# Turning the linear queries and the local queries ahead of the linear keys, and projecting attention's output ahead of the MLP's first output products

## The chip, the cores and the metric

One core of a Trainium2 chip runs the whole program. The metric is the device time of one execution in microseconds; a kernel's time is the median of several runs. Five engines work side by side and wait for each other by semaphores: TensorE (PE; its weight loads are shown apart as PEld), VectorE (DVE), ScalarE (ACT), GpSimd (POOL) and SyncE (SP), which starts the DMAs.

## What is computed

The input is 4096 tokens of 256 numbers. Two things are computed from the normalised input and put together:

```python
xn = layernorm(x)
# linear attention, 16 heads of 32, in chunks of 128 tokens with a carried state
q, k = softmax(ln(xn) @ Wq + bq), softmax(ln(xn) @ Wk + bk)      # per head
v, p = split(ln(xn) @ W_in)
k = (1 - smear) * k + smear * k_previous_token
attn = tril((q / s) @ (k / s).T * decay_mask)
s_out = ln(silu(p) * (attn / attn.sum()) @ v @ W_out)
# two layers of local attention (8 heads of 64, windows of 128) with a gated MLP
for l in range(2):
    q, k, v = split(shift(x) @ wqkv[l])
    q, k = rotary(l2norm(q) * qs, l2norm(k) * ks)
    x = x + softmax(local q @ k.T) @ v @ wo[l]
    h = layernorm(shift(x)) * g + b
    a, gate = split(h @ w1[l] + b1[l]); x = x + (a * gelu(gate)) @ w2[l] + b2[l]
out = x_in + s_out * silu(x)
```

## The kernel before

Work is cut into windows of 128 tokens; 32 windows in each of two layers make 64 units. The program is a software pipeline of 67 iterations. Iteration i projects unit i (queries, keys, values of the local attention), attends for unit i-1 and runs the MLP of unit i-2; in layer 1 a last stage finishes unit i-3. The linear attention is spread over the same iterations, one chunk of 128 tokens for every two of them: an odd iteration runs its first part (`one`: projections, softmax, turning queries and keys, scores), the even one behind it the second (`two`: outputs, state, gate, output projection). So every odd iteration from 1 to 63 has a `one`, 32 in all. Most iterations run in loops of two bodies each, an even and an odd one.

Every engine has its own queue, with the order written out by hand in a function `body` for each; an engine takes the next instruction only when the one before has been issued and its waits are met. `Steps` counts an engine's signals: the names are in the order in which they are given, and `at(name, unit)` is the count to wait for.

A matmul wants its contracted index on the partitions, so queries and keys are turned by TensorE (`transposes`, L1530, four blocks of 128x128 into one PSUM bank; the profile shows them under L1533) and copied to SBUF by ScalarE (`copy`, shown under L793). At the end of an odd iteration TensorE's order is:

1. the linear keys into `mix_bank[0]`, waiting for `kadd` (L1431 on VectorE: this token's share of the keys plus that of the token before, both in `mix_work`) and `v`;
2. the local queries (`turn_q`), waiting for `rot` (L1421, the rotation's sum) and for ScalarE's copy of the values out of the same bank (`v_loc`);
3. the linear queries into `mix_bank[1]`, waiting for the softmax's exponentials;
4. two of the six output products of the MLP (`mlp_out(m, 0, 2)`, tiles `w_s`, `hid`), waiting for `a0` (L1279 on VectorE, `gated`);
5. the output projection of the local attention (`out_projection`, tiles `wo_s`, `oT`), waiting for `lb` (L1236);
6. the local keys (`turn_k`), waiting for `knorm` (L1443, the rotated keys times their inverse norms) and for `ql` (L1243, the low half of the turned local queries, which frees the bank);
7. the linear scores, the other MLP products, and the next unit's x.

VectorE's order over the same time is `kadd`, `lb`, `gated`, `knorm`, `ql`, in layer 0 the statistics of the next x, the MLP's last gates (L1132), `residual` (L1124, reads the output projection), `kl` (L1243 on kT, behind ScalarE's copy of the turned local keys), then the linear scores' decays and, in the next iteration, the local scores (L1048). GpSimd's order is `k_dec` (L738, waits for `kadd`), in layer 0 up to iteration 30 the root of the next x's norm (`norm1`, L755), `qT_dec` (L758, waits for ScalarE's copy of the turned linear queries), the root for the local queries' norms (L663) and `x1b` (L767). `qT_dec` is read by the next iteration's linear outputs.

Of the kernel before, what the change touches and what calls it, by code (L numbers as in the profile page):

```python
# [30 lines left out]
P = 128  # L31
# [14 lines left out]
MG = ME // P  # L46
# [126 lines left out]
def build(nc, x_d, in_w, in_b, q_w, q_b, k_w, k_b, out_w, out_b, W_in, W_out, Wq, bq, Wk, bk,  # L173
# [9 lines left out]
    with ExitStack() as ctx:  # L183
        def sb(name, shape):
            return ctx.enter_context(nc.sbuf_tensor(name, shape, F32))
# [7 lines left out]
        def sem(name):  # L193
            return ctx.enter_context(nc.semaphore(name))
# [52 lines left out]
        qk = mix_work[:, 0:2 * ME]  # L247
# [9 lines left out]
        qT_mix = sb("qT_mix", [P, MG, P])  # L257
# [5 lines left out]
        kT_mix = sb("kT_mix", [P, MG, P])  # L263
# [59 lines left out]
        mix_bank = bank[0:2]  # L323
# [4 lines left out]
        score_bank = [mix_bank[0], mix_bank[1], att_bank[0], att_bank[2]]  # L328


        mix_pe = Steps(sem("mix_pe"), "q k v kt qt s0 s1 s2 s3 p o0 o1 gt wout")
        state_pe = Steps(sem("state_pe"), "st0 st1")
        state_dve = Steps(sem("state_dve"), "st0 st1")
        state_pool = Steps(sem("state_pool"), "sdec")
        rows_pe = Steps(sem("rows_pe"), "xt")
        rows_dve = Steps(sem("rows_dve"), "xl")
        mix_act = Steps(sem("mix_act"), "xt exp kt qt tanh gt")
        mix_dve = Steps(sem("mix_dve"), "q k max sum kinv kw v kadd "
                        "s2 qsum qeps s3 s0 s1 p den0 rec0 o0 den1 rec1 o1 go "
                        "ystat yaggr yvar")  # L340
# [101 lines left out]
        def linear(i):  # L442


            odd, n = i.c == 1, i.low // 2
            return (Chunk(i.k, n) if odd and n < NW else None,
                    Chunk(i.k - 1, n - 1) if not odd and 1 <= n < NW + 1 else None,
                    Chunk(i.k - 1, n - 1) if odd and 1 <= n < NW + 1 else None)
# [6 lines left out]
        def streams(i):  # L455

            return (i if i.low < UNITS else None,
                    i.back(1) if 1 <= i.low < UNITS + 1 else None,
                    i.back(2) if 2 <= i.low < UNITS + 2 else None,
                    i.back(3) if i.low >= NW + 3 else None)  # L460
# [330 lines left out]
        def _(act):  # L791
            def copy(out, in_):
                return act.activation(out, in_, ACT.Copy)  # L793
# [75 lines left out]
            def body(i):  # L869
                proj, a, m, f = streams(i)  # L870
                one, two, y = linear(i)
# [92 lines left out]
                if m is not None:  # L964
                    last_gates(m)
                if one is not None:
                    act.wait_ge(mix_pe.sem, mix_pe.at("kt", one))
                    copy(kT_mix[:, :, :], mix_bank[0][:, :].rearrange("p (g i) -> p g i", g=MG))\
                        .then_inc(mix_act.done("kt"), 1)
                if proj is not None:  # L970
                    act.wait_ge(proj_pe.sem, proj_pe.at("qt", proj))
                    copy(halved(qT[:, 0, :, :]), proj_bank[:, :].rearrange("p (g i) -> p g i", g=HP))\
                        .then_inc(proj_act.done("qt"), 1)
                if one is not None:
                    act.wait_ge(mix_pe.sem, mix_pe.at("qt", one))
                    copy(qT_mix[:, :, :], mix_bank[1][:, :].rearrange("p (g i) -> p g i", g=MG))\
                        .then_inc(mix_act.done("qt"), 1)
                if proj is not None:
                    act.wait_ge(proj_pe.sem, proj_pe.at("kt", proj))
                    copy(halved(kT[:, 0, :, proj.parity, :]), proj_bank[:, :].rearrange("p (g i) -> p g i", g=HP))\  # L980
# [7 lines left out]
                if one_next is not None:  # L988
                    turned_rows(one_next)

            iterations(act, body)


# [525 lines left out]
        def _(pe):  # L1519
            def mm(out, lhsT, rhs, first, last):  # L1520
                return pe.matmul(out, lhsT, rhs, start=first, stop=last)  # L1521

            def mm3(out, left, right, first, last):

                for n, (a, b) in enumerate(((1, 0), (0, 1), (0, 0))):
                    ins = pe.matmul(out, halved(left[:, a]), halved(right[:, b]), start=first and n == 0,  # L1526
                                    stop=last and n == 2)
                return ins

            def transposes(out, parts):  # L1530

                for j, part in enumerate(parts):
                    ins = pe.transpose(out[:, j * P:(j + 1) * P], part, ident)  # L1533
                return ins
# [72 lines left out]
            def hidden(m, b, at, first, count):  # L1607

                for j in range(count):
                    for c in range(DC):  # L1610
                        ins = mm(b[:, (at + j) * P:(at + j + 1) * P], w1_s[:, c, (first + j) * P:(first + j + 1) * P],
                                 hT_n[:, c, :], c == 0, c == DC - 1)
                return ins

            def out_projection(a, b):
                if window(a).low == 0:
                    pe.wait_ge(setup_dve.sem, setup_dve.at(f"wo_{layer(a)}", ONCE))
                pe.wait_ge(att_dve.sem, att_dve.at("lb", a))
                for g in range(HP):
                    ins = mm3(b[:, 0:D], oT[:, :, g, :], wo_s[:, :, g, :], g == 0, g == HP - 1)  # L1620
                ins.then_inc(att_pe.done("wo"), 1)

            def turn_q(u):

                pe.wait_ge(proj_act.sem, proj_act.at("v", u))
                pe.wait_ge(proj_dve.sem, proj_dve.at("rot", u))
                transposes(proj_bank, [rot[:, g * P:(g + 1) * P] for g in range(HP)])\
                    .then_inc(proj_pe.done("qt"), 1)
# [33 lines left out]
            def mlp_out(m, first, last):  # L1662

                if first == 0:
                    if window(m).low == 0:
                        pe.wait_ge(w2_loaded, 16 * W2_DMAS * (layer(m) + 1))
                    pe.wait_ge(mlp_dve.sem, mlp_dve.at("a0", m))
                if last > 4:
                    pe.wait_ge(mlp_dve.sem, mlp_dve.at("ga", m))
                for j in range(first, last):  # L1670
                    ins = mm(mlp_bank[1][:, 0:D], hid[:, j, :], w2_s[:, j, :], j == 0, j == HC - 1)
                if last == HC:
                    ins.then_inc(mlp_pe.done("w2"), 1)
# [42 lines left out]
            def body(i):  # L1716
                u, a, m, f = streams(i)
                one, two, y = linear(i)
# [91 lines left out]
                if m is not None and one is None and i.low != UNITS:  # L1810
                    mlp_out(m, 0, 2)
                if one is not None:
                    pe.wait_ge(mix_dve.sem, mix_dve.at("kadd", one))
                    pe.wait_ge(mix_dve.sem, mix_dve.at("v", one))
                    transposes(mix_bank[0], [qk[:, ME + g * P:ME + (g + 1) * P] for g in range(MG)])\
                        .then_inc(mix_pe.done("kt"), 1)
                if u is not None:
                    turn_q(u)
                if one is not None:
                    pe.wait_ge(mix_act.sem, mix_act.at("exp", one))  # L1820
                    pe.wait_ge(mix_dve.sem, mix_dve.at("k", one))
                    transposes(mix_bank[1], [qk[:, g * P:(g + 1) * P] for g in range(MG)])\
                        .then_inc(mix_pe.done("qt"), 1)
                    if m is not None:
                        mlp_out(m, 0, 2)
                if a is not None:
                    out_projection(a, att_bank[1])
                if i.low == UNITS:

                    hidden(m, mlp_bank[0], 2, 4, 2).then_inc(mlp_pe.done("ga"), 1)  # L1830
                    mlp_out(m, 0, 2)
# [24 lines left out]
                if two is not None:  # L1856
# [10 lines left out]
                    ins.then_inc(mix_pe.done("wout"), 1)  # L1867

            iterations(pe, body)


# [23 lines left out]
```

## Time and profile before

| | |
|---|---|
| median of 3 runs | 1975.97 us (1974.36 to 1982.03) |
| the profiled execution | 1983.42 us |
| its span, first to last instruction | 1981.6 us |
| TensorE busy | 1906.0 us, 96% |
| VectorE busy | 1732.8 us, 87% |
| ScalarE busy | 1224.2 us, 62% |
| GpSimd busy | 1018.6 us, 51% |

Busy time counts an instruction from its start to its end; instructions of one engine overlap by some hundredths of a microsecond at their edges. A bracket behind a row of the timeline is the time for which the engine sat idle before it, and what ended that. The profile is of one execution, the median of others, so times inside the span are compared with the profiled execution.

### The profile page before, as it was taken

The numbers are of one execution on the slowest core, as the hardware profiler recorded it, in microseconds if no ns is written. First come the engines' busy times: TensorE is split into PE (matmuls) and PEld (weight loads), VectorE is DVE, ScalarE is ACT, GpSimd is POOL, SyncE is SP. The second block draws the span as 40 slices with busy tenths as digits, with TensorE's granted clock in tenths as the row PEclk, the third lists the DMA queues.
The fourth block names the chain that finished last, engine by engine and source line by source line (L and its number), as shares of the span: only waits on it lengthen the run. The fifth ranks groups of instructions, "written<-read, shape, count | busy, mean of one in ns | idle before, by whom it ended". The sixth has DMA issues, their size and how long they took to land.

```text
span 1981.6 us, 49031 instructions
## 1 busy us (share of the span) xinstructions
PE 1906.0 (96%) x15178; PEld 1645.8 (83%) x15178; DVE 1732.8 (87%) x5212; ACT 1224.2 (62%) x2926; POOL 1018.6 (51%) x1004
## 2 busy tenths in 40 slices
PE   5899999999999999999999999999999999999998
PEld 3788888888888888888788888888888888888887
DVE  5888899898889898889888898889899898898896
ACT  4565656656656656656666567566566566566564
POOL 2545555556556555555444455454554554454552
PEclk8999999999999999999999999999999999999999
DMA  5010000000000100000111111110111111111101
GB/s 199 20 33 21 29 25 22 30 29 22 25 29 21 32 29 21 26 26 25 65 62 47 40 34 41 34 32 29 42 32 40 37 32 29 40 34 34 37 26 33
DMA packets 81152, 72.76 MB, mean 37 GB/s; under 512 B 13484, under 2 KB 74344, under 8 KB 81096
## 3 DMA queue, kind: packets, MB, share of 16 engines
q1 hardware_dynamic: 81096, 72.05, 11.8%
q8 instruction: 31, 0.51, 0.1%
q14 instruction: 25, 0.20, 0.0%
HBM read 42.64 MB, written 16.78 MB: 30 GB/s over the span
## 4 chain that ended last, share of the span: by engine, by line
PE 61%; issue 12%; DVE 12%; ACT 6%; POOL 6%; DVEq 1%; DMA 1%; SPq 0%; POOLq 0%; ACTq 0%
PE bank L1521 36%; PE bank L1526 14%; PE bank L1533 10%; ACT L944 2%; POOL rot_other L707 2%; PE bank L1568 2%; POOL mix_work L715 2%; DVE rot L1413 1%; DVE prob L1048 1%; ACT gel L944 1%; DVE mix_work L1431 1%; POOL small_h L663 1%; DVE sq_sum L1305 1%; POOL small_y L663 1%; DVE mix_work L1112 1%
## 5 line engine op out<-in xcount | busy, mean ns | idle before, releaser
L1521 PE MATMUL bank<-hT_n,w_s 128*128 128x128 f32 x3072 | 402.2, 281 | 1.6 <-ACT hT_n L907 0.9
L1521 PEld LDWEIGHTS bank<-hT_n,w_s 128*128 128x128 f32 x3072 | 364.7, 191 | 35.2 <-issue 21.4
L824 ACT ACTIVATE prob<-prob,row_min 128x256 f32<-128x256 f32 x512 | 256.7, 504 | 171.2 <-DVE row_min L1048 169.6
L1526 PE MATMUL bank<-wqkv_s,xT 128*128 128x512 f32 x1152 | 319.2, 413 | 4.6 <-DVE wqkv_s L1225 1.8
L663 POOL TENSOR_TENSOR inv_norm<-sq_clip,half_neg 128x8 f32<-128x8 f32 x128 | 270.3, 2112 | 55.5 <-DVE sq_clip L1308 55.4
L707 POOL TENSOR_TENSOR rot_other<-raw,rot_t 128x256 f32<-128x256 f32 x256 | 190.2, 774 | 150.0 <-ACT raw L793 150.0
L1526 PEld LDWEIGHTS bank<-wqkv_s,xT 128*128 128x128 f32 x1152 | 207.4, 191 | 53.6 <-DVE wqkv_s L1225 3.8
L1048 DVE CUSTOM_DVE_ANT_0 prob<-bank,table,inv_norm 128x256 f32<-128x256 f32 x512 | 226.5, 479 | 3.9 <-issue 3.6
L1521 PE MATMUL bank<-w_s,hid 128*128 128x256 f32 x768 | 202.3, 387 | 0.0
L793 ACT ACTIVATE pT<-bank 128x512 f32<-128x512 f32 x256 | 139.7, 606 | 30.3 <-PE bank L1533 30.2
L1533 PE MATMUL bank<-table,prob 128*128 128x128 f32 x1024 | 144.9, 274 | 2.3 <-DVE prob L1067 2.3
L1521 PE MATMUL bank<-pT,v_loc 128*64 128x128 f32 x2048 | 140.1, 279 | 5.4 <-ACT pT L793 4.9
L1521 PEld LDWEIGHTS bank<-w_s,hid 128*128 128x128 f32 x768 | 131.5, 191 | 14.7 <-DVE hid L1279 0.2
L1067 DVE TENSOR_SCALAR prob<-prob,row_inv 128x256 f32<-128x256 f32 x384 | 134.1, 391 | 6.8
L1568 PEld LDWEIGHTS bank<-kT,qT 64*128 64x128 f32 x1536 | 100.1, 187 | 45.9 <-issue 29.9
L663 POOL TENSOR_TENSOR small_h<-small_h,half_neg 128x1 f32<-128x1 f32 x64 | 35.4, 553 | 190.3 <-DVE small_h L1292 190.3
L1521 PEld LDWEIGHTS bank<-pT,v_loc 128*64 128x64 f32 x2048 | 109.3, 136 | 23.3 <-issue 9.1
L1568 PE MATMUL bank<-kT,qT 64*128 64x256 f32 x1536 | 126.3, 297 | 1.3 <-DVE row_min L1048 1.0
L793 ACT ACTIVATE oT<-bank 128x256 fp32r<-128x256 f32 x128 | 50.1, 391 | 124.0 <-PE bank L1521 124.0
L1533 PEld LDWEIGHTS bank<-table,prob 128*128 128x128 f32 x1024 | 119.7, 143 | 8.1 <-DVE prob L1067 2.8
L1521 PE MATMUL bank<-v_mix,mix_work 128*128 128x33 f32 x1024 | 124.8, 266 | 0.0
L1521 PEld LDWEIGHTS bank<-v_mix,mix_work 128*128 128x128 f32 x1024 | 124.5, 191 | 0.0
(180 smaller groups left out, 4313.6 us busy)
## 6 DMA issues: line engine op xcount, KB each, us to landing
k_prev<-k_carry SPq DMA_DIRECT2D x32, 224.0 KB, 2.5
x_s<-in_L_attn_x SPq DMA_DIRECT2D x32, 128.0 KB, 2.1
rot_s<-in_rotary SPq DMA_DIRECT2D x64, 64.0 KB, 2.0
rows_normalised<-xh SPq DMA_DIRECT2D x32, 128.0 KB, 1.7
y_n<-rows_normalised SPq DMA_DIRECT2D x32, 128.0 KB, 2.1
x_between_layers<-x SPq DMA_DIRECT2D x32, 128.0 KB, 1.7
s_between_passes<-s_out SPq DMA_DIRECT2D x32, 128.0 KB, 1.7
x_s<-x_between_layers SPq DMA_DIRECT2D x32, 128.0 KB, 2.1
```

Source lines behind the costliest of these rows:

```text
L663: return pool.tensor_tensor(out, in_, half_neg[:, 0:w], ALU.pow)
L707: ins = pool.tensor_tensor(o5[:, a, :, s, :], r5[:, a, :, 1 - s, :], rot_t[:, 2 + a, s, :].unsqueeze(1).to_broadcast([P, H, HD // 2]), ALU ...
L715: pool.tensor_tensor(qk_h, qk_h, qk_max[:, :].unsqueeze(2).to_broadcast([P, 2 * MH, MD]), ALU.subtract).then_inc(mix_pool.done("sub"), 1)
L793: return act.activation(out, in_, ACT.Copy)
L824: ins = act.activation(prob[:, h, :], prob[:, h, :], ACT.Exp, bias=row_min[:, c:c + 1], scale=-1.0, accum_out=row_sum[:, c:c + 1])
L944: ins = act.activation(gel[:, j, :], mlp_bank[0][:, j * P:(j + 1) * P], ACT.Gelu, bias=bias[:, HC + j:HC + j + 1])
L1048: ins = dve.tensor_tensor_reduce(prob[:, h, :], b[:, j * 2 * P:(j + 1) * 2 * P], mask, inv_norm[:, a.parity, h:h + 1], 3e38, ALU.add, ALU.min,
L1067: ins = dve.tensor_scalar(prob[:, h, :], prob[:, h, :], row_inv[:, c:c + 1], None, ALU.mult)
L1521: return pe.matmul(out, lhsT, rhs, start=first, stop=last)
L1526: ins = pe.matmul(out, halved(left[:, a]), halved(right[:, b]), start=first and n == 0, stop=last and n == 2)
L1533: ins = pe.transpose(out[:, j * P:(j + 1) * P], part, ident)
L1568: ins = pe.matmul(banks[s][:, j * 2 * P:(j + 1) * 2 * P], halved(qT[rows, lo_q, h // 2, :]), halved(kT[rows, lo_k, h // 2, :, :].rearrange ...
```

## The change

TensorE turns the linear queries first, then the local queries, then the linear keys. The two MLP output products that stood behind the linear queries in an odd iteration now stand behind the output projection. ScalarE copies the turned tiles out in the new order, and the two signal lists name them so. Nothing is added or left out; even iterations keep their order.

```diff
--- before.py
+++ after.py
@@ -328,13 +328,13 @@
         score_bank = [mix_bank[0], mix_bank[1], att_bank[0], att_bank[2]]
 
 
-        mix_pe = Steps(sem("mix_pe"), "q k v kt qt s0 s1 s2 s3 p o0 o1 gt wout")
+        mix_pe = Steps(sem("mix_pe"), "q k v qt kt s0 s1 s2 s3 p o0 o1 gt wout")
         state_pe = Steps(sem("state_pe"), "st0 st1")
         state_dve = Steps(sem("state_dve"), "st0 st1")
         state_pool = Steps(sem("state_pool"), "sdec")
         rows_pe = Steps(sem("rows_pe"), "xt")
         rows_dve = Steps(sem("rows_dve"), "xl")
-        mix_act = Steps(sem("mix_act"), "xt exp kt qt tanh gt")
+        mix_act = Steps(sem("mix_act"), "xt exp qt kt tanh gt")
         mix_dve = Steps(sem("mix_dve"), "q k max sum kinv kw v kadd "
                         "s2 qsum qeps s3 s0 s1 p den0 rec0 o0 den1 rec1 o1 go "
                         "ystat yaggr yvar")
@@ -964,17 +964,17 @@
                 if m is not None:
                     last_gates(m)
                 if one is not None:
-                    act.wait_ge(mix_pe.sem, mix_pe.at("kt", one))
-                    copy(kT_mix[:, :, :], mix_bank[0][:, :].rearrange("p (g i) -> p g i", g=MG))\
-                        .then_inc(mix_act.done("kt"), 1)
+                    act.wait_ge(mix_pe.sem, mix_pe.at("qt", one))
+                    copy(qT_mix[:, :, :], mix_bank[1][:, :].rearrange("p (g i) -> p g i", g=MG))\
+                        .then_inc(mix_act.done("qt"), 1)
                 if proj is not None:
                     act.wait_ge(proj_pe.sem, proj_pe.at("qt", proj))
                     copy(halved(qT[:, 0, :, :]), proj_bank[:, :].rearrange("p (g i) -> p g i", g=HP))\
                         .then_inc(proj_act.done("qt"), 1)
                 if one is not None:
-                    act.wait_ge(mix_pe.sem, mix_pe.at("qt", one))
-                    copy(qT_mix[:, :, :], mix_bank[1][:, :].rearrange("p (g i) -> p g i", g=MG))\
-                        .then_inc(mix_act.done("qt"), 1)
+                    act.wait_ge(mix_pe.sem, mix_pe.at("kt", one))
+                    copy(kT_mix[:, :, :], mix_bank[0][:, :].rearrange("p (g i) -> p g i", g=MG))\
+                        .then_inc(mix_act.done("kt"), 1)
                 if proj is not None:
                     act.wait_ge(proj_pe.sem, proj_pe.at("kt", proj))
                     copy(halved(kT[:, 0, :, proj.parity, :]), proj_bank[:, :].rearrange("p (g i) -> p g i", g=HP))\
@@ -1810,21 +1810,21 @@
                 if m is not None and one is None and i.low != UNITS:
                     mlp_out(m, 0, 2)
                 if one is not None:
+                    pe.wait_ge(mix_act.sem, mix_act.at("exp", one))
+                    pe.wait_ge(mix_dve.sem, mix_dve.at("k", one))
+                    transposes(mix_bank[1], [qk[:, g * P:(g + 1) * P] for g in range(MG)])\
+                        .then_inc(mix_pe.done("qt"), 1)
+                if u is not None:
+                    turn_q(u)
+                if one is not None:
                     pe.wait_ge(mix_dve.sem, mix_dve.at("kadd", one))
                     pe.wait_ge(mix_dve.sem, mix_dve.at("v", one))
                     transposes(mix_bank[0], [qk[:, ME + g * P:ME + (g + 1) * P] for g in range(MG)])\
                         .then_inc(mix_pe.done("kt"), 1)
-                if u is not None:
-                    turn_q(u)
-                if one is not None:
-                    pe.wait_ge(mix_act.sem, mix_act.at("exp", one))
-                    pe.wait_ge(mix_dve.sem, mix_dve.at("k", one))
-                    transposes(mix_bank[1], [qk[:, g * P:(g + 1) * P] for g in range(MG)])\
-                        .then_inc(mix_pe.done("qt"), 1)
-                    if m is not None:
-                        mlp_out(m, 0, 2)
                 if a is not None:
                     out_projection(a, att_bank[1])
+                if m is not None and one is not None:
+                    mlp_out(m, 0, 2)
                 if i.low == UNITS:
 
                     hidden(m, mlp_bank[0], 2, 4, 2).then_inc(mlp_pe.done("ga"), 1)
```

## Rows read from the trace of the kernel before

**Rows 1.** The page: its first line, and busy time by engine.

```profile
span 1981.6 us, 49031 instructions
...
PE 1906.0 (96%) x15178; PEld 1645.8 (83%) x15178; DVE 1732.8 (87%) x5212; ACT 1224.2 (62%) x2926; POOL 1018.6 (51%) x1004
```

**Rows 2.** Stages: one loop turn of layer 0, one of layer 1; us, busy (instructions).

```profile
848.33:908.19 59.86, 58.93 (x474) 51.08 (x474) 53.57 (x169) 37.63 (x91) 32.95 (x33) 1.00 0.09 26
...
1453.00:1513.10 60.10, 58.83 (x474) 51.05 (x475) 53.81 (x158) 38.10 (x92) 30.83 (x29) 1.00 0.12 35
```

**Rows 3.** Table of waits: us in total, times, longest us.

```profile
PEld bank L1533 <- DVE mix_work L1431: 40.4, 32, 4.1
```

**Rows 4.** The chain that ended last, around one wait: start us, us, what.

```profile
907.52 0.69 DVE mix_work L1431
...
908.34 1.52 PE bank L1533 x12
```

**Rows 5.** Timeline, layer 0, weight loader: start us, us, engine, line, work.

```profile
908.33 0.42 PEld L1533 LDWEIGHTS bank<-table,mix_work 128*128 128x128 f32 x4 [0.89 <-DVE mix_work L1431]
...
909.15 0.47 PEld L1533 LDWEIGHTS bank<-table,mix_work 128*128 128x128 f32 x4
...
909.63 0.73 PEld L1521 LDWEIGHTS bank<-w_s,hid 128*128 128x128 f32 x4
...
910.38 1.58 PEld L1526 LDWEIGHTS bank<-wo_s,oT 128*128 128x128 f32 x12
...
911.91 0.46 PEld L1533 LDWEIGHTS bank<-table,rot 128*128 128x128 f32 x4
```

**Rows 6.** Timeline, the same iteration: VectorE, ScalarE, and the loader at the second scores.

```profile
906.38 1.23 DVE L1421 TENSOR_TENSOR rot<-rot,rot_other 128x1024 f32<-128x1024 f32 x1
...
906.87 0.59 ACT L793 ACTIVATE v_loc<-bank 128x512 f32<-128x512 f32 x1
...
908.12 0.42 DVE L1236 TENSOR_TENSOR oT<-bank,oT 128x256 fp32r<-128x256 f32 x1
...
908.46 1.12 DVE L1279 SCALAR_TENSOR_TENSOR hid<-bank,cols,gel 128x128 f32<-128x128 f32 x4
...
910.14 0.69 DVE L1243 TENSOR_TENSOR qT<-bank,qT 128x512 fp32r<-128x512 f32 x1
...
911.52 0.61 DVE L1132 SCALAR_TENSOR_TENSOR hid<-bank,cols,gel 128x128 f32<-128x128 f32 x2
...
912.21 0.42 DVE L1124 TENSOR_TENSOR x<-bank,xn 128x256 f32<-128x256 f32 x1
...
913.27 0.69 DVE L1243 TENSOR_TENSOR kT<-bank,kT 128x512 fp32r<-128x512 f32 x1 [0.64 <-ACT kT L793]
...
918.28 0.77 PEld L1568 LDWEIGHTS bank<-kT,qT 64*128 64x128 f32 x12 [0.36 <-DVE row_min L1048]
```

**Rows 7.** Timeline, a steady odd iteration of layer 1: loader, GpSimd and VectorE.

```profile
1513.10 0.42 PEld L1533 LDWEIGHTS bank<-table,mix_work 128*128 128x128 f32 x4 [1.25 <-DVE mix_work L1431]
...
1513.13 1.05 POOL L738 TENSOR_TENSOR k_dec<-mix_work,table 128x512 f32<-128x512 f32 x1 [0.51 <-DVE mix_work L1431]
...
1514.26 0.68 DVE L1443 TENSOR_TENSOR rot<-rot,inv_norm 128x512 f32<-128x512 f32 x1
...
1514.91 0.69 DVE L1243 TENSOR_TENSOR qT<-bank,qT 128x512 fp32r<-128x512 f32 x1
...
1515.45 0.74 POOL L758 TENSOR_TENSOR qT_dec<-qT_mix,table 128x256 f32<-128x256 f32 x1 [1.27 <-ACT qT_mix L793]
...
1516.14 1.65 POOL L663 TENSOR_TENSOR inv_norm<-sq_clip,half_neg 128x8 f32<-128x8 f32 x1
1516.70 0.46 PEld L1533 LDWEIGHTS bank<-table,rot 128*128 128x128 f32 x4
```

**Rows 8.** Timeline, an even iteration of layer 0: GpSimd and VectorE at L1443.

```profile
877.99 1.06 POOL L751 TENSOR_TENSOR state<-state,table 128x528 f32<-128x528 f32 x1
...
878.29 1.30 DVE L1443 TENSOR_TENSOR rot<-rot,inv_norm 128x512 f32<-128x512 f32 x1
```

## Prediction

> **What bounds the kernel now.** I read the page first: TensorE is busy 96% of a span of 1981.6 us [rows 1]. So a gain has to be idle time taken from TensorE, or work taken from it, and the change takes no work away: the same instructions stand in another order. Next the table of stages, one loop turn (an even and an odd iteration) of each layer: 59.86 us a turn in layer 0, 60.10 in layer 1, TensorE busy 58.93 and 58.83 [rows 2]. About one microsecond a turn is left. The table of waits says where most of it lies: the weight loader sat 40.4 us in 32 waits before the transposes of L1533, for the write of mix_work by L1431 [rows 3]. L1431 is VectorE's "kadd", the sum of the linear keys; it is there once per odd iteration, so every one of the 32 waits is the wait in front of the linear keys' transposes. The chain that ended last runs through the same place, from kadd straight into these transposes [rows 4]. So the wait is on the path and has to be taken seriously, all the more as VectorE, ScalarE and GpSimd lead up to it without slack.
>
> **Layer 0, TensorE.** In a steady odd iteration [rows 5] the loader idles 0.89 us until 908.33; its last group before the wait has ended at 907.44. Behind the wait stand three groups of four transposes (linear keys, local queries, linear queries), then two of the MLP's output products at 909.63, the output projection at 910.38 and the turn of the local keys at 911.91. The change puts the linear queries and the local queries ahead of the wait. What they need is there: the exponentials and the projection of the linear queries are long done; the local queries' rotation ends at 906.38 + 1.23 = 907.61, and the copy of v_loc, which freed their bank, at 907.46 [rows 6]. The linear keys still cannot start before 908.33, since kadd is unmoved. So the gain is not the 0.89 of idle time but the two groups that no longer stand behind it: 909.15 - 908.33 = 0.82 us. Two groups take 0.82 and the issue gap in front of them ends some 0.05 to 0.15 after 907.44, so they end at 908.31 to 908.41: they may push the keys by up to 0.08. I take 0.77, with 0.72 and 0.82 as ends.
>
> After the keys (0.48 us, 909.15 to 909.63) the output projection begins at about 908.81. It waits for "lb", VectorE's low half of the second attention result, ready at 908.12 + 0.42 = 908.54: no wait. The MLP products follow at about 910.34 (the projection takes 911.91 - 910.38 = 1.53); their "a0" is ready at 908.46 + 1.12 = 909.58. Had they kept their place ahead of the projection they would have met a0 at 908.81 and waited 0.77 us, which would have eaten the gain; this is what the second part of the change is worth, and it costs nothing itself, since the MLP products write another bank and the next of them come only behind the linear scores. The local keys follow 0.75 later at 911.09. They need "ql" on VectorE, which ends at 910.14 + 0.69 = 910.83: just in time, 0.26 us of cover [rows 6].
>
> **Layer 0, VectorE.** A gain of TensorE's is kept only if VectorE can give it too. From 913.27 on it is without a gap, and TensorE waits for it at the second scores (0.36 idle at 918.28) [rows 6]. Between kadd and 913.27 it idles 0.08 us for the output projection (from 911.52 + 0.61 to 912.21) and 0.64 us for ScalarE's copy of the turned local keys (913.27), which itself follows the transposes that now come 0.77 earlier. Earlier by 0.77 the copy ends at about 912.47, and VectorE, done with the residual at 912.55 or 0.07 before it with the overlap of starts that its rows show, goes on at once. So VectorE gives 0.72 plus the overlap: 0.77 goes through. The running maximum, the decays, the next x and the next scores are all behind these on the same queue and move with them; the even iteration behind it is TensorE's own.
>
> **Layer 1, the same and a collision.** The wait is longer (1.25 on the loader at 1513.10, [rows 7]), but the keys again start no earlier than kadd allows, so the saving is again the two groups, 0.82. What differs is GpSimd. Its queue is k_dec (L738), then in layer 0 the root of the next x's norm (waits for VectorE until late), then qT_dec (L758). From iteration 31 on there is no such root. Now qT_dec waits for the linear queries' copy and starts at 1515.45. After the change that copy comes ahead of the keys', near 1513.3, so qT_dec starts as soon as k_dec ends: 1513.13 + 1.05 = 1514.18, or some 0.03 before it, as the back-to-back rows at 1515.45 and 1516.14 overlap. VectorE's scaling of the local keys (L1443) starts at 1514.26, and reads two tiles in SBUF as qT_dec does. The trace shows what that does [rows 8]: at 878.29 the same L1443 began 0.30 us after a GpSimd operation (877.99 for 1.06) and took 1.30 instead of 0.68, as if it had stood until 878.91, 0.14 before GpSimd's operation ended. Behind qT_dec (1514.15 for 0.74) it would stand until 1514.75 and end at 1515.43 instead of 1514.94, 0.49 later. The Trainium skill has this as the shared port pair (SBUF — State Buffer, Who interferes with whom): a VectorE instruction with two SBUF inputs and a GpSimd one that reads SBUF exclude each other for the whole instruction; here the row agrees but for the 0.14, and by the page the delay would be 0.63 and the whole gain some 2 us less. L1443 delayed, "ql" behind it (1514.91, 0.69) ends at 1516.09. TensorE would have come to the local keys at 1516.70 - 0.82 = 1515.88; it goes on 0.06 behind ql, at about 1516.15 to 1516.2. The saving in layer 1 shrinks from 0.82 to **0.52**. Ends: 0.82 if the two miss each other (the margin is 0.11 us), 0.37 if the delay is the longer.
>
> **The sum.** Odd iterations with the root in between: 1 to 29, 15 of them, at 0.77: 11.6 us. Without it: 31 to 63, 17 of them, at 0.52: 8.8 us. Together 20.4 us. The first few iterations wait longer, but the cap of two groups holds for them too. The profiled execution took 1983.42 us (span 1981.6 and 1.8 around it); 1963.0 after, a ratio of 0.9897. The runs' median, 1975.97, is 0.4% below the profiled one; by the ratio it becomes **1955.6 us**.
>
> **Rivals.**
> - *The two operations miss each other in layer 1* (or L1443 wins the port, and GpSimd waits, which costs nothing as qT_dec is needed only in the next iteration). 15 x 0.77 + 17 x 0.82 = 25.5 us: 1950.6. For it: 0.11 us of margin is little. Against: both starts follow from kadd, by fixed durations.
> - *VectorE keeps layer 0's gain.* If residual or the key copy don't come earlier (ScalarE held by its new order of copies), the wait at the second scores grows from 0.36 to over 1.1 us and layer 0 gives nothing: 8.8 us in all, 1967.2, within 0.5%. Against: ScalarE idles before the keys' copy, and its three copies of 0.6 us fit between 908.3 and 910.1. A gain partly lost, 10 us, is the same case.
> - *Slower: L1443 is held through both GpSimd operations.* If the root of 1.65 us that follows qT_dec (1516.14) takes the port first as well, L1443 stands until 1514.15 + 0.74 + 1.65 - 0.14 = 1516.40 and ends at 1517.08; ql behind it ends near 1517.75, and the local keys turn at 1517.8, 1.1 us later than before. 17 x 1.1 - 11.6 = 7 us slower: 1983. It costs layer 1 from a delay of L1443 of about 1.04 on (ql later than 1516.64) and outweighs layer 0's gain from about 1.7 on (1.04 and 11.6 us over 17). Against it: in [rows 8] L1443 got in after one operation, though such a root was next.
>
> **How the numbers follow.** Two medians of this kernel can be told apart from about 0.5%, 9.9 us. Chances: the forecast 0.55 (1952 to 1961), no collision 0.20 (1948 to 1953), VectorE or another engine keeping half or more 0.17 (1962 to 1973), slower 0.05 (1976 to 1990); 0.03 for a gain above 28 us. Leaving out the far ends, the range is 1947.5 to 1968. Faster by over 0.5% (under 1966.1) takes the first two, the surprise and part of the third: 0.83; within 0.5% 0.14; slower 0.03.
>
> **What would show it.** Right: the loader's wait for L1431 falls from 0.89 to below 0.1 us in layer 0 and from 1.25 to some 0.2 in layer 1; the order on TensorE is transposes of mix_work, rot, mix_work, then wo_s, then hid; L1443 takes about 1.17 us in layer 1's odd iterations and 0.68 in layer 0's, and the loader shows a new wait of about 0.3 us for "ql" (qT, L1243) there; a turn takes 59.1 us in layer 0 and 59.6 in layer 1. Wrong: L1443 at 0.68 throughout (then 1950), a wait before the output projection or at the second scores grown by the whole gain, or kadd itself later against the start of its turn, which nothing moved should cause.

## The result

The changed kernel takes 1958.85 us in the median of 4 runs (1955.28 to 1959.92), the kernel before 1977.12 us in runs beside it: a ratio of 0.9902, 95% interval 0.9877 to 0.9926. A second comparison, the same changed kernel on another occasion, gives 1958.05 us and 0.9881 (0.9866 to 0.9896). The forecast was 1955.6 us and a ratio of 0.9897. Of all runs in this document one was slow: e2's at 2101.97 us, at a granted clock of 0.849 where the others have 0.994 to 0.997; its ratio leaves that run out, its median counts it.

The profiled execution has a span of 1958.1 us, 23.5 less than the 1981.6 of [rows 1]. The two lines of its page that answer to those show TensorE's busy time all but unchanged and a shorter span around it:

```profile
span 1958.1 us, 49031 instructions
...
PE 1906.7 (97%) x15178; PEld 1637.0 (84%) x15178; DVE 1741.4 (89%) x5212; ACT 1223.2 (62%) x2926; POOL 1025.9 (52%) x1004
```

The stages, one loop turn of layer 0 and one of layer 1, with the columns of [rows 2]. The turns are 0.62 and 0.64 us shorter, and VectorE's busy time in layer 1 has grown from 53.81 to 54.12:

```profile
835.66:894.90 59.24, 58.81 (x477) 50.94 (x475) 53.66 (x168) 37.51 (x91) 32.94 (x33) 1.00 0.09 27
1435.52:1494.98 59.46, 59.20 (x475) 50.83 (x475) 54.12 (x158) 38.15 (x94) 31.25 (x30) 1.00 0.12 35
```

In the table of waits, the wait for VectorE's L1243 (ql) has grown from 7.3 us in 32 waits (first row), and the one of [rows 3] has shrunk from 40.4 us to a sixth (second row):

```profile
PEld bank L1533 <- DVE qT L1243: 15.1, 50, 1.7
...
PEld bank L1533 <- DVE mix_work L1431: 6.3, 16, 1.3
```

The timeline of a steady odd iteration of layer 0, to be read against [rows 5, 6]. Kadd (L1431) starts at 894.06, and times are best read from there:

```profile
893.90 0.47 PEld L1533 LDWEIGHTS bank<-table,mix_work 128*128 128x128 f32 x4
...
894.06 0.68 DVE L1431 TENSOR_TENSOR mix_work<-mix_work,k_prev 128x512 f32<-128x512 f32 x1
...
894.34 0.47 PEld L1533 LDWEIGHTS bank<-table,rot 128*128 128x128 f32 x4
...
894.87 0.42 PEld L1533 LDWEIGHTS bank<-table,mix_work 128*128 128x128 f32 x4
...
895.25 1.48 PEld L1526 LDWEIGHTS bank<-wo_s,oT 128*128 128x128 f32 x12
...
896.66 0.74 PEld L1521 LDWEIGHTS bank<-w_s,hid 128*128 128x128 f32 x4
...
897.43 0.57 PEld L1533 LDWEIGHTS bank<-table,rot 128*128 128x128 f32 x4
...
898.91 0.69 DVE L1243 TENSOR_TENSOR kT<-bank,kT 128x512 fp32r<-128x512 f32 x1
...
900.95 0.73 POOL L767 TENSOR_TENSOR x1b<-x,b_s 128x256 f32<-128x256 f32 x1
901.21 0.50 DVE L1484 TENSOR_TENSOR q_eps<-qk_sum,head_eps 128x16 f32<-128x16 f32 x1
...
905.24 1.22 PEld L1526 LDWEIGHTS bank<-win_s,xhT 128*128 128x128 f32 x6 [0.55 <-DVE mix_work L1112]
```

The linear queries and the local queries are turned while kadd runs, and the keys follow at +0.81 (894.87), exactly where they stood before (908.33 against 907.52) and without a wait. The local keys' turn starts at +3.37 instead of +4.39, the linear scores behind it at +4.11 instead of +5.01, VectorE's kT at +4.85 instead of +5.75. The row of the scores, before and after:

```profile
912.53 0.98 PEld L1521 LDWEIGHTS bank<-qT_mix,kT_mix 32*128 32x128 f32 x32 [0.17 <-issue]
```

```profile
898.17 0.98 PEld L1521 LDWEIGHTS bank<-qT_mix,kT_mix 32*128 32x128 f32 x32 [0.17 <-issue]
```

Then comes a row that was not forecast: q_eps (L1484), 16 numbers a row, takes 0.50 us instead of 0.17. It began at 901.21, inside GpSimd's x1b (L767, 900.95 to 901.68). The linear projection behind the second scores, at 905.24, waits 0.55 us for VectorE, where before it waited 0.25 (at 919.30).

The same stretch in layer 1, against [rows 7]:

```profile
1494.27 0.42 PEld L1533 LDWEIGHTS bank<-table,rot 128*128 128x128 f32 x4 [0.19 <-DVE rot L1421]
...
1494.94 0.42 PEld L1533 LDWEIGHTS bank<-table,mix_work 128*128 128x128 f32 x4 [0.26 <-DVE mix_work L1431]
...
1494.98 1.05 POOL L738 TENSOR_TENSOR k_dec<-mix_work,table 128x512 f32<-128x512 f32 x1 [0.52 <-DVE mix_work L1431]
...
1495.99 0.73 POOL L758 TENSOR_TENSOR qT_dec<-qT_mix,table 128x256 f32<-128x256 f32 x1
1496.11 1.16 DVE L1443 TENSOR_TENSOR rot<-rot,inv_norm 128x512 f32<-128x512 f32 x1
1496.68 2.10 POOL L663 TENSOR_TENSOR inv_norm<-sq_clip,half_neg 128x8 f32<-128x8 f32 x1
...
1497.19 0.68 DVE L1243 TENSOR_TENSOR qT<-bank,qT 128x512 fp32r<-128x512 f32 x1
...
1497.92 0.42 PEld L1533 LDWEIGHTS bank<-table,rot 128*128 128x128 f32 x4 [0.41 <-DVE qT L1243]
```

The forecast collision is there: qT_dec starts 0.04 before k_dec's end, L1443 begins 0.12 behind it and takes 1.16 us instead of 0.68, and TensorE waits 0.41 us for ql before it can turn the local keys. The wait for kadd (L1431) is 0.26 us, and a short new one of 0.19 stands before the local queries, for the rotation's sum (L1421).

In layer 0 the chain that ended last has left TensorE between kadd and the next iteration. Before, it ran from kadd into the transposes [rows 4]; now it stays on VectorE (start us, us, what):

```profile
894.06 0.14 DVE mix_work L1431
...
895.08 0.82 DVE hid L1279 x4
...
896.03 0.68 DVE rot L1443
896.71 0.60 DVE qT L1243
...
898.61 0.33 DVE x L1124
...
901.21 0.06 DVE q_eps L1484
```

### The profile page after: what moved, and what is told of

It is laid out like the page before. It is cut to its first block, busy times and chain, and to the rows that moved or that the text cites. A ratio compares the mean times of both kernels' runs of the same rounds, so it can differ in the third digit from the quotient of the medians.

```text
span 1958.1 us, 49031 instructions
## 1 busy us (share of the span) xinstructions
PE 1906.7 (97%) x15178; PEld 1637.0 (84%) x15178; DVE 1741.4 (89%) x5212; ACT 1223.2 (62%) x2926; POOL 1025.9 (52%) x1004
## 4 chain that ended last, share of the span: by engine, by line
PE 56%; DVE 16%; issue 13%; ACT 6%; POOL 6%; DVEq 1%; DMA 1%; SPq 0%; POOLq 0%; ACTq 0%
PE bank L1521 34%; PE bank L1526 13%; PE bank L1533 9%; ACT L944 2%; POOL rot_other L707 2%; POOL mix_work L715 2%; PE bank L1568 2%; DVE prob L1048 2%; DVE rot L1413 1%; ACT gel L944 1%; DVE mix_work L1111 1%; DVE mix_work L1112 1%; POOL small_h L663 1%; DVE sq_sum L1305 1%; POOL small_y L663 1%
## 5 line engine op out<-in xcount | busy, mean ns | idle before, releaser
L663 POOL TENSOR_TENSOR inv_norm<-sq_clip,half_neg 128x8 f32<-128x8 f32 x128 | 279.5, 2184 | 52.9 <-DVE sq_clip L1308 52.8
```

The costliest lines, as they stand in the source:

```text
L663: return pool.tensor_tensor(out, in_, half_neg[:, 0:w], ALU.pow)
```

## The experiments

A turn is the time from one start of k_dec (L738) to the next. The table has the steady turns of the profiled executions, and the first turn (iteration 1 to 3). Each ratio is to runs of the kernel before from the same occasion: their median was 1980.33 us beside e1 to e4 and 1980.40 beside e5 to e8, so medians of different occasions are not to be divided by each other.

| kernel | first | layer 0 | layer 1 | median us | ratio (95%) |
|---|---|---|---|---|---|
| before | 62.48 | 59.85 | 60.10 | 1977.12 | 1 |
| before, again (e5) | 62.53 | 59.86 | 60.13 | 1981.08 (1 run) | |
| changed | 59.76 | 59.24 | 59.46 | 1958.85 | 0.9902 (0.9877 to 0.9926) |
| changed, again (e6) | 59.78 | 59.25 | 59.48 | 1958.05 | 0.9881 (0.9866 to 0.9896) |
| turns only (e1) | 60.98 | 59.87 | 60.13 | 1977.7 | 0.9987 (0.9974 to 0.9999) |
| projection only (e2) | 62.49 | 59.83 | 60.10 | 1979.26 | 0.9993 (0.9978 to 1.0007) |
| changed, x1b first (e3) | 59.75 | 58.96 | 59.23 | 1949.03 | 0.9842 (0.982 to 0.9863) |
| changed, root first (e4) | 59.80 | 59.25 | 59.23 | 1954.01 | 0.9867 (0.9846 to 0.9888) |
| before, wait filled (e7) | 59.67 | 59.86 | 60.13 | 1976.58 | 0.9979 (0.9969 to 0.9988) |
| before, x1b first (e8) | 60.42 | 59.85 | 60.10 | 1980.88 | 1.0 (0.9991 to 1.0009) |

### Each half of the change alone

The turns in the new order, the MLP products in their old place. Against the changed kernel:

```diff
-                if a is not None:
-                    out_projection(a, att_bank[1])
                 if m is not None and one is not None:
                     mlp_out(m, 0, 2)
+                if a is not None:
+                    out_projection(a, att_bank[1])
```

> Only the three turns are in the new order; the two MLP products stay ahead of the output projection. Theory (the two halves need each other): the linear keys still start 0.8 us after kadd's start, the MLP products come 0.4 us later and wait some 0.8 us for their first gate products (hid, L1279), so the local keys' turn starts 4.4 us after kadd's start as in the kernel before, and a steady turn takes 59.85 us in layer 0 and 60.1 in layer 1. Only the first turns gain, up to 5 us in all: ratio 0.997 to 1.000. Rival (the new order of the turns is the whole gain, the place of the MLP products is of no matter): turns of 59.2 and 59.5 us, ratio 0.990.

The steady turns did not move at all (59.87 and 60.13). The weight loader's rows in an odd iteration of layer 0, whose kadd starts at 659.59:

```profile
660.40 0.42 PEld L1533 LDWEIGHTS bank<-table,mix_work 128*128 128x128 f32 x4
...
661.70 0.73 PEld L1521 LDWEIGHTS bank<-w_s,hid 128*128 128x128 f32 x4 [0.88 <-DVE hid L1279]
...
663.99 0.46 PEld L1533 LDWEIGHTS bank<-table,rot 128*128 128x128 f32 x4
```

The keys are turned at +0.81 and the products come 0.88 us of waiting later, for the gated products (hid, L1279); the local keys' turn starts at +4.40, where [rows 5] have it (+4.39). The whole gain of the two turns is given back in one wait. In layer 1, L1443 is stretched in this run too (1.15 us), and it costs nothing: ql ends at kadd + 3.73, and TensorE reaches the local keys at + 4.41 anyway.

The other half, in the kernel before:

```diff
                     transposes(mix_bank[1], [qk[:, g * P:(g + 1) * P] for g in range(MG)])\
                         .then_inc(mix_pe.done("qt"), 1)
-                    if m is not None:
-                        mlp_out(m, 0, 2)
                 if a is not None:
                     out_projection(a, att_bank[1])
+                if m is not None and one is not None:
+                    mlp_out(m, 0, 2)
```

> Only the output projection goes ahead of the MLP's first products; the turns keep their old order. Theory (it gives nothing by itself, since TensorE has the same work behind the same wait): turns of 59.7 to 59.85 and 60.0 to 60.1 us, the output projection's 12 loads about 0.1 us shorter as in the changed kernel, ratio 0.998 to 1.000. Rival (the earlier residual is what VectorE needed): VectorE's idle time in front of the residual goes, and a turn gets 0.3 us or more shorter, ratio 0.995 or less.

It gives nothing that can be told from nothing. So neither half has a steady gain, and both together have 0.6 us a turn: the first frees the time, the second lets TensorE use it.

### Taking the collisions away

GpSimd's x1b ahead of qT_dec, in the changed kernel. The edit moves qT_dec and the root that follows it behind x1b:

```diff
                 if i.low + 1 < NW:
                     norm1(i.back(-1))
-                if one is not None:
-                    pool.wait_ge(mix_act.sem, mix_act.at("qt", one))
-                    pool.tensor_tensor(qT_dec[:, :, :], qT_mix[:, 0:MG // 2, :], query_decay,
-                                       ALU.mult).then_inc(mix_pool.done("qdec"), 1)
-                if proj is not None and one is not None:
-
-                    root(inv_norm[:, proj.parity, 0:H], sq_clip[:, 0:H], H).then_inc(proj_pool.done("invq"), 1)
                 if att_u is not None:
                     if window(att_u).low == 0:
...
                     pool.tensor_tensor(x1b[:, att_u.parity, :], x1[:, att_u.parity, :], b2_s[:, :],
                                        ALU.add).then_inc(att_pool.done("x1b"), 1)
+                if one is not None:
+                    pool.wait_ge(mix_act.sem, mix_act.at("qt", one))
+                    pool.tensor_tensor(qT_dec[:, :, :], qT_mix[:, 0:MG // 2, :], query_decay,
+                                       ALU.mult).then_inc(mix_pool.done("qdec"), 1)
+                if proj is not None and one is not None:
+
+                    root(inv_norm[:, proj.parity, 0:H], sq_clip[:, 0:H], H).then_inc(proj_pool.done("invq"), 1)
```

(The dots are between the two places of the edit.)

> The changed kernel, and on GpSimd x1b goes ahead of qT_dec in the odd iterations, so qT_dec no longer starts at the end of k_dec, and x1b no longer runs when VectorE computes q_eps. Theory (both layers lose to GpSimd and VectorE reading SBUF at once: L1443 behind qT_dec in layer 1, q_eps behind x1b in layer 0): L1443 back at 0.68 us everywhere in odd iterations, L1484 back at 0.17; a turn of 58.95 us in layer 0 (0.30 shorter) and 59.2 in layer 1 (0.25 shorter), 8 to 9 us less than the changed kernel, ratio to the kernel before 0.986. Rival (the two long rows are a consequence of waits, and VectorE or the loop's chain sets the turn): turns stay at 59.24 and 59.46, ratio 0.990.

Both rows went back and both turns came as expected, 58.96 and 59.23. GpSimd and q_eps in layer 0, and below them the row of one turn:

```profile
658.95 0.73 POOL L760 TENSOR_TENSOR x1b<-x,b_s 128x256 f32<-128x256 f32 x1 [0.33 <-DVE x L1124]
...
659.64 0.83 POOL L764 TENSOR_TENSOR qT_dec<-qT_mix,table 128x256 f32<-128x256 f32 x1
...
660.43 1.65 POOL L663 TENSOR_TENSOR inv_norm<-sq_clip,half_neg 128x8 f32<-128x8 f32 x1
...
661.18 0.17 DVE L1484 TENSOR_TENSOR q_eps<-qk_sum,head_eps 128x16 f32<-128x16 f32 x1
```

```profile
832.00:890.96 58.96, 58.75 (x477) 50.98 (x475) 53.38 (x168) 37.53 (x91) 33.09 (x34) 1.00 0.09 27
```

x1b is over by 659.68, q_eps at 661.18 lies inside the root instead, and it takes 0.17 again. This version beats both kernels: 1949.03 us, 9 to 10 us under the changed one's two medians, which were taken on other occasions. The steady turns give 15 x 0.28 + 17 x 0.23 = 8.1 us of it, and the turn across the layers takes 63.61 us instead of 64.29 (e6).

One collision of this kind stays in all the kernels here: in layer 0's even iterations L1443 takes 1.30 us beside GpSimd's L751 [rows 8], in e3 too. Nothing was tried on it.

Only the root ahead of qT_dec, x1b in its place:

```diff
+                if proj is not None and one is not None:
+
+                    root(inv_norm[:, proj.parity, 0:H], sq_clip[:, 0:H], H).then_inc(proj_pool.done("invq"), 1)
                 if one is not None:
                     pool.wait_ge(mix_act.sem, mix_act.at("qt", one))
...
-                if proj is not None and one is not None:
-
-                    root(inv_norm[:, proj.parity, 0:H], sq_clip[:, 0:H], H).then_inc(proj_pool.done("invq"), 1)
```

> The changed kernel, and on GpSimd the root for the local queries goes ahead of qT_dec in the odd iterations; x1b keeps its place. Theory: only layer 1's collision is gone (L1443 at 0.68, its turn near 59.2 us), as the root reads only 8 numbers a row; layer 0's stays (L1484 at 0.50, turn 59.24), so 4 us less than the changed kernel, ratio 0.988. Rival (any GpSimd operation that starts before L1443 holds it until it ends): the root of 1.65 us holds L1443 longer than qT_dec did, L1443 takes 2 us or more and layer 1's turn gets longer than 60 us.

Layer 1 gains its 0.23 us (59.23), layer 0 keeps its 59.25 and its q_eps of 0.46 to 0.57 us (0.73 in iteration 1). Together, e3 and e4 put a price on each collision. In layer 1:

```profile
1492.82 1.65 POOL L663 TENSOR_TENSOR inv_norm<-sq_clip,half_neg 128x8 f32<-128x8 f32 x1
1492.93 0.68 DVE L1443 TENSOR_TENSOR rot<-rot,inv_norm 128x512 f32<-128x512 f32 x1
...
1494.43 0.73 POOL L761 TENSOR_TENSOR qT_dec<-qT_mix,table 128x256 f32<-128x256 f32 x1
```

The root starts 0.11 us ahead of L1443 and lasts 1.65 us, and L1443 takes its plain 0.68. An operation that began earlier does not hold VectorE as such: this one reads 8 numbers a row, where qT_dec reads 256 from each of two tiles. It is also another kind of operation, a power and not a product; which of the two spares L1443, no run separates. With this the slower rival, L1443 held through the root too, has nothing left.

The control, e3's edit in the kernel before:

> The kernel before with GpSimd's x1b ahead of qT_dec in the odd iterations, the edit of e3 without the change. Theory (the collisions that e3 took away were made by the change): turns of 59.85 and 60.1 us as in the kernel before, L1443 at 0.68 and L1484 at 0.17 as they were, ratio 0.998 to 1.001. Rival (GpSimd's order gives the kernel before the same 0.3 us a turn): 59.55 and 59.85, ratio 0.995.

Ratio 1.0 (0.9991 to 1.0009): L1443 and q_eps are at 0.68 and 0.17 in its odd iterations, as in the kernel before. That kernel had no collision there to lose; the changed one made both.

### The first turns

The first profile showed more gain in the first three turns than the order explains: they took 62.48, 61.30 and 61.45 us, and 59.76, 59.33 and 59.24 after. Both kernels were profiled again, unchanged.

> The kernel before, unchanged, profiled a second time. It asks which part of the changed kernel's gain in its first turns belongs to the order and which to the one execution. Theory: the first turn's 62.5 us comes again (a wait of 4 us on TensorE, then the granted clock at 0.50), and turns two and three, 61.2 and 61.5 us in the first profile behind a late k_prev DMA, come at 59.9. Rival: all three come again (62.5, 61.2, 61.5), so the order takes 5 us of waits out of the start.

> The changed kernel, unchanged, again. Theory: turns of 59.24 and 59.46 us and 59.8 in the first, L1484 at 0.50 in layer 0 and L1443 at 1.16 in layer 1; the turn across the layers is 63.7 to 64.3 us where the weights land earlier than in the first profile (65.55, with the clock at 0.57 for 4 us behind a wait of 2.8), ratio 0.988 to 0.990. Rival: 65.55 comes again, and the order costs a microsecond there.

Of the kernel before, only the first long turn came again (62.53, then 59.98 and 59.85). Turns two and three of the first profile were that execution's: in iteration 5 kadd waited 1.26 us for k_prev's DMA, TensorE idled 2.24 us for kadd, and its granted clock was 0.59 from 189.90 to 193.75. The changed kernel's second profile had one such turn too (60.64, behind a wait of 1.37 us for kadd). The turn across the layers was 65.55 us in the first profile of the changed kernel and 64.29 in the second, against 64.24 and 64.30 before: the order gains nothing in it. There TensorE's wait for the second layer's weights (wqkv_s, L1225) took 1.73 us before, 2.79 and 2.52 in the two profiles after; behind the 2.79 the granted clock was 0.57 from 964.20 to 968.20, behind the 2.52 it was 1.00.

The first turn's 2.7 us came again in both pairs. Behind the wait of 4.06 us in iteration 1 the kernel before runs slow:

```profile
64.79 0.71 PEld L1533 LDWEIGHTS bank<-table,mix_work 128*128 128x128 f32 x4 [4.06 <-DVE mix_work L1431]
65.49 0.87 PEld L1533 LDWEIGHTS bank<-table,rot 128*128 128x128 f32 x4
...
67.19 2.68 PEld L1526 LDWEIGHTS bank<-wo_s,oT 128*128 128x128 f32 x12
```

```profile
64.80:66.90 2.10, 2.10 (x10) 2.10 (x11) 1.61 (x2) 0.70 (x2) 1.05 (x1) 0.50 0.01 1
```

Four weight loads take 0.87 us where [rows 5] have 0.47, twelve take 2.68 instead of 1.58, at a granted clock of 0.50 (the last but two columns). The changed kernel runs at 1.00 behind this place. It does not idle much less here; the turns that were pulled ahead cut its idle time into pieces of 0.17, 1.79 and 1.26 us:

```profile
61.07 0.42 PEld L1533 LDWEIGHTS bank<-table,mix_work 128*128 128x128 f32 x4 [0.17 <-issue]
...
63.29 0.42 PEld L1533 LDWEIGHTS bank<-table,rot 128*128 128x128 f32 x4 [1.79 <-issue]
...
64.97 0.42 PEld L1533 LDWEIGHTS bank<-table,mix_work 128*128 128x128 f32 x4 [1.26 <-DVE mix_work L1431]
```

To test that it is the clock, the kernel before was given useless work in the wait, in iteration 1 only:

```diff
+                if i.low == 1:
+                    pe.wait_ge(mix_dve.sem, mix_dve.at("k", one))
+                    for _ in range(7):
+                        transposes(mix_bank[1], [ident] * 4)
                 if one is not None:
                     pe.wait_ge(mix_dve.sem, mix_dve.at("kadd", one))
```

> The kernel before; in iteration 1 alone TensorE turns the identity 28 times into a bank that is overwritten afterwards, while it waits for kadd. Theory (the first turn is long because TensorE idled 4 us and its clock then fell to 0.50): the granted clock stays at 1.00 behind the wait, the three turns behind it take 0.43 us each instead of 0.87, and the first turn takes 60.9 us or less instead of 62.5; ratio 0.999. Rival (the first turn is long by its data's lateness, not by the clock): 62.5 again, or longer by the added work.

```profile
57.77 2.29 PEld L1533 LDWEIGHTS bank<-table 128*128 128x128 f32 x21 [0.33 <-issue]
...
60.79 0.47 PEld L1533 LDWEIGHTS bank<-table,mix_work 128*128 128x128 f32 x4
...
62.10 1.49 PEld L1526 LDWEIGHTS bank<-wo_s,oT 128*128 128x128 f32 x12
```

```profile
60.00:64.00 4.00, 4.00 (x38) 4.00 (x36) 3.27 (x8) 1.58 (x3) 1.14 (x2) 1.00 0.01 1
```

(The first row is of a stretch that ends at 60 us and has 21 of the 28 transposes; all 28 take 3.05 us.) The clock is 1.00 behind the wait, the loads take 0.47 and 1.49 us, the first turn 59.67. The kernel with 28 more transposes is faster, ratio 0.9979 (0.9969 to 0.9988). In this execution k_dec, which waits for kadd, started at 60.40 us and not at 64.81. The start itself varies like this: k_dec began at 60.4 to 60.8 us in e1, e7 and e8, and at 64.5 to 65.3 in the other seven profiles. The fair comparison is e8, with k_dec at 60.83 and the wait (2.83 us) unfilled: there the granted clock fell to 0.50 from 62.0 on and the first turn took 60.42. So the fill is worth 0.75 us in an early start. Its first turn is 2.8 us shorter than those of the late starts, but no late start was profiled with the fill, so it isn't shown that the clock is all of that. The medians differ by 3.8 us (1976.58 against 1980.40), more than the 0.999 expected and more than the first turn explains; where the rest comes from stays open. For the same reason the order's 2.7 us hold for late starts; no early start of the changed kernel was profiled.

## Why the prediction held, and where it did not

**The place and the mechanism: right.** The keys start at kadd + 0.81 in every kernel; what was gained is the work that no longer stands behind them. MLP products ahead of the projection would have waited: forecast 0.77 us, measured 0.88 in e1, and the second half of the change is worth nothing alone (e2) and everything beside the first (e1).

**The step "two groups that no longer stand behind it, 0.82": too small.** I subtracted 909.15 - 908.33, which are the first two of three groups, and the group right behind the wait is the short one (0.39). The one behind it starts at:

```profile
908.72 0.47 PEld L1533 LDWEIGHTS bank<-table,rot 128*128 128x128 f32 x4
```

The two that leave take 909.63 - 908.72 = 0.91, and TensorE reaches the linear scores 0.90 earlier after kadd than before. With the collisions gone (e3) the turns are 0.89 and 0.87 us shorter than before. The deduction of up to 0.1 for late keys was not needed: the loader's gap was used to the end, and the keys start on time.

**Layer 0, "0.77 goes through": wrong, 0.61.** What I missed is the second collision. I placed GpSimd's x1b nowhere in layer 0's timeline. It starts when the root before it ends, at kadd + 6.9, before and after alike, as its chain runs from VectorE's statistics of the next x, which the change doesn't move. q_eps did move, from kadd + 8.05, behind x1b, to + 7.15, into it. It lost 0.33 us on a queue that I had rightly found to have no gap, and TensorE's wait for VectorE behind the second scores grew by 0.30. e3 gives it back: 0.28 us a turn, e4 leaves it.

**Layer 1, the collision: right in place and form.** L1443 forecast at 1.17 us, measured 1.16; a wait of "about 0.3 us" for ql, measured 0.41. The gain was 0.64 instead of 0.52. It is set by the end of ql and not by the size of the saving: ql ended at kadd + 3.73 where I had + 3.80, and TensorE went on 0.05 behind it, at + 3.78, where I had about + 3.89. The saving, larger than I took it, only made the wait for ql longer (0.41). The rival that the two operations miss each other fell (L1443 is at 1.08 to 1.17 in all 17 iterations without norm1), and e4 and e3 show what it would have given, some 0.25 us a turn.

**The sum: right by errors that cancel, which is luck.** Forecast were 15 x 0.77 + 17 x 0.52 = 20.4 us. The second pair of profiles (e5 and e6) shows what made up the gain: 13 steady turns of layer 0 gave 7.9 us in all (0.61 each), 15 turns of layer 1 gave 10.0 (0.67 each), the turn across the layers nothing, and the first turn 2.75; the changed kernel's late DMA took 0.7 back in the second. That is 20.05, and with the start and the end of the program the spans differ by 20.9. So layer 0 gave less than forecast and layer 1 more. "The cap of two groups holds for the first few iterations too" was wrong for the first, whose long wait also cost clock; and the turn across the layers, counted like any other, gave nothing. The first pair's 23.5 contain late DMAs on both sides. The medians went down by 18.3 us in the first comparison and 22.4 in the second, so they don't tell the sum more closely than that.

**VectorE keeps layer 0's gain: partly true**, though not by the route that I gave (ScalarE's new order of copies). ScalarE's copies of queries and keys were in time. The chain in layer 0 is VectorE's now.

## What to carry to other kernels

When the first instruction behind a wait cannot start earlier, the gain of pulling others ahead of it is the length of these others, not the idle time; and the one behind them must be ready too, or the gain turns into its wait. Look then at what moves against what does not, on VectorE and GpSimd, whose operations stretched each other here where both read SBUF: in layer 0 q_eps came 0.9 us earlier and x1b stayed, in layer 1 qT_dec came earlier and L1443 stayed, and pairs that had missed each other by 0.4 to 0.5 us met. The fix was an order on GpSimd's queue that did nothing for the kernel before.

## What the runs showed of the hardware

- A VectorE tensor_tensor with both inputs in SBUF stretches beside a GpSimd tensor_tensor that reads SBUF, by about what is left of the GpSimd operation when it begins, less 0.13 or 0.14 us: L1443 by 0.48 (qT_dec had 0.61 to go), q_eps by 0.33 (x1b had 0.47 to go), though q_eps itself has only 16 numbers a row. In [rows 8] the same L1443 lost 0.62 (L751 had 0.76 to go). GpSimd loses too: the root behind qT_dec took 2.10 us instead of 1.65, beside an L1443 that had 0.59 to go when it began, again less 0.14.
- The GpSimd operation's duration alone does not give the price: the root of 1.65 us on 8 numbers a row, started 0.11 us earlier, cost L1443 nothing (e4), and q_eps, inside the same root in e3, took its 0.17. The Trainium skill (SBUF — State Buffer, SBUF: two separate sides) has the one that starts first hold the shared port pair for the whole instruction. The rows of qT_dec and x1b agree but for 0.13 and 0.14 us, the root's does not.
- TensorE's granted clock fell to 0.50 behind the loader's waits of 4.06 us (kernel before) and 2.83 (e8), and was 0.57 and 0.59 in the mean of some 4 us behind 2.79 and 2.24. It was 1.00 behind waits of 1.77 and 1.26, but also behind 2.39 (kernel before, at 57.67) and 2.52 (e6, at 965.23), and in e8 it was 0.69 from 54 to 56 us behind one of 2.38. So the length of the last wait alone does not say whether the clock falls. In e1, whose wait for kadd in iteration 1 was 1.08, it fell to 0.50 from 69.4 to 71.4 behind several waits of 0.5 to 0.8 between 65 and 68 us; that turn took 60.98.
- 28 useless transposes in the wait of iteration 1 left the clock at 1.00 behind it, where without them (e8) it fell to 0.50, and the kernel came out 0.2% faster (0.9979, 0.9969 to 0.9988).
